# Attention by head pairs: both heads' scores side by side on TensorE, the softmax division moved behind the value product, and the batch loop written out

## What is computed

```
h = tok(x)                                   # Xnew[n] = sum over t of Wt[t, n] * x[t]
h = h + attn(layernorm(h))                   # attn normalises its input once more
h = h + ffn(layernorm(h))

xn  = (x - mu) / sqrt(var + 1e-05) * gamma + beta
q, k, v = three projections, each followed by a 3-tap convolution along the tokens
sim = q @ k.T - slope[head] * abs(i - j), masked to j <= i
out = softmax(sim) @ v
return out @ wout.T
```

## Time and profile before

| what | us |
|---|---|
| median of three runs | 1566.63 |
| the profiled execution's own time | 1568.55 |
| its span, first to last instruction | 1566.8 |
| PE busy in the span | 1354.8 |
| PE weight loads | 1089.1 |
| DVE busy | 952.7 |
| ACT busy | 671.4 |
| POOL busy | 264.4 |

### The profile page before, as it was taken

How to read it: one execution, slowest core, us unless ns; L and a number is a source line. 1 busy time by engine, 2 the same in 40 slices (tenths; PEclk the granted TensorE clock), 3 DMA queues, 4 the chain that set the end, 5 groups by cost and what they waited for, 6 DMA issues and landing times. The chain is left out here.

```text
span 1566.8 us, 26688 instructions
## 1 busy us (share of the span) xinstructions
PE 1354.8 (86%) x7905; PEld 1089.1 (70%) x7905; DVE 952.7 (61%) x3107; ACT 671.4 (43%) x1759; POOL 264.4 (17%) x262
## 2 busy tenths in 40 slices
PE   6999999999369999989999899999997896466663
PEld 5999999999356777766767667677665685355553
DVE  3433434334569898879878798788874566621211
ACT  2334334333235655656546565456653341021211
POOL 6000000000010001001110000100000400178885
PEclk9999999999679999999999999999998898687877
DMA  4000000000100000000000000000000112044542
GB/s 106 17 15 20 20 10 20 20 10 20 35 11 10 2 22 23 22 21 17 10 17 21 21 20 10 14 21 12 12 12 20 28 34 60 6 79 81 97 82 39
DMA packets 93851, 43.86 MB, mean 28 GB/s; under 512 B 31295, under 2 KB 90088, under 8 KB 93752
## 3 DMA queue, kind: packets, MB, share of 16 engines
q1 hardware_dynamic: 69960, 36.25, 8.5%
q0 software_dynamic: 23808, 6.69, 3.3%
HBM read 29.52 MB, written 10.18 MB: 25 GB/s over the span
## 5 line engine op out<-in xcount | busy, mean ns | idle before, releaser
L783 ACT ACTIVATE P<-P,nmax 125x375 f32<-125x375 f32 (+2 forms) x384 | 189.1, 494 | 292.1 <-DVE nmax L923 291.9
L287 PE MATMUL bank<-h1hl,W2hl 128*128 128x376 f32 x1536 | 278.0, 336 | 2.9 <-DVE h1hl L402 2.9
L287 PEld LDWEIGHTS bank<-h1hl,W2hl 128*128 128x128 f32 x1536 | 264.0, 189 | 3.1 <-DVE h1hl L402 3.1
L624 PE MATMUL bank<-QK 64*125 64x375 f32 (+2 forms) x768 | 197.8, 391 | 13.4 <-DVE nmax L923 13.4
L624 PEld LDWEIGHTS bank<-QK 64*125 64x125 f32 x768 | 112.8, 185 | 75.8 <-DVE nmax L923 25.0
L364 ACT ACTIVATE h<-bank,b2c 128x375 f32<-128x375 f32 x128 | 73.5, 574 | 207.3 <-PE bank L287 207.3
L923 DVE CUSTOM_DVE_ANT_0 P<-bank,nbias 125x375 f32<-125x375 f32 (+2 forms) x384 | 139.7, 413 | 2.6 <-PE bank L624 2.5
L1569 ACT ACTIVATE hE<-bank,EB 128x375 f32<-128x375 f32 x64 | 36.7, 573 | 199.0 <-PE bank L1544 196.4
L680 PE MATMUL bank<-WVT,xnThl 128*125 128x512 f32 x432 | 115.7, 413 | 3.0 <-DVE QK L972 3.0
L913 DVE TENSOR_SCALAR P<-P,prec 125x375 f32<-125x375 f32 (+2 forms) x384 | 111.9, 347 | 4.5
L865 POOL TENSOR_SCALAR lnve<-lnmv 125x3 f32<-125x3 f32 x32 | 10.1, 315 | 575.6 <-DVE lnmv L891 575.6
(11 more groups left out here) (196 smaller groups left out, 2363.4 us busy)
## 6 DMA issues: line engine op xcount, KB each, us to landing
X<-in_x_dram SPq DMA_DIRECT2D x34, 375.0 KB
EW<-in_L_ffn_w_dram SPq DMA_DIRECT2D x32, 256.0 KB
token_table<-row SPq DMA_DIRECT2D x16, 210.9 KB
tTall<-tT SPq DMA_DIRECT2D x16, 187.5 KB, 2.3
out_dram<-oS SPq DMA_DIRECT2D x16, 187.5 KB
tTall<-in_L_tok_W_dram SPq DMA_DIRECT2D x1, 1024.0 KB, 7.1
EB<-in_L_ffn_b_dram SPq DMA_DIRECT2D x16, 62.5 KB
tok<-token_table,ids POOLq DMA_INDIRECT x48
```

The costliest lines, as they stand in the source:

```text
L287: last = nc.tensor.matmul(bank[4 + m % 2][:, :NE], W2hl[:, a, k, m * 128:(m + 1) * 128], h1hl[:, p, b, k], start=(k == 0 and n == 0), stop ...
L624: last = nc.tensor.matmul(bS[unit][:PT_, at:at + w], QK[r:r + DH, 0, c, i * PT_:(i + 1) * PT_], QK[r:r + DH, 1, c, :w], start=True, stop=True)
L783: nc.scalar.activation(P[:, h % 4, SEG[q]:SEG[q] + w], P[:, h % 4, SEG[q]:SEG[q] + w], ACT.Exp, bias=nmax[:, h % 4, q:q + 1], scale=-1.0, ...
```

## The change

Attention now goes by pairs of heads. A body still has eight steps, two for each pair c = h // 2: part 0 has the 375-wide score block of both heads, part 1 the 250- and the 125-wide blocks of both. In each, the matmul of the even head (array rows 0 to 63, bank bS[0]) is followed by that of the odd head (rows 64 to 127, bank bS[1]).

`P` is no longer multiplied by the reciprocal. The six row sums of a pair get one small reciprocal (`prec`, 6 elements a row), which a copy widens over 64 channels and both heads (`precw`, 384 elements). PE transposes `precw` with three more transposes per pair into columns 375 to 499 of the bT banks, ScalarE copies them into `PT` with the probabilities, and DVE multiplies the attended values by them when it takes them out of bO into `OT`; ScalarE's copy of bO is gone. All four copies of transposed probabilities of a pair are ScalarE's now, three of them 500 wide. The transposes read 128 columns of `P` where they read 125. They and `attend` stand one pair and two pairs behind the scores.

The two norms in a row before the attention become one with a combined variance term; `n1`, nine instructions on it and six of its statistics are gone. GpSimd subtracts and multiplies for both remaining norms (two 384-element operations each) and computes `cellmax`, which has two buffers now. The loop in `bodies` is gone: b = -3 to 17 is straight code, and waits are on constants.

Cut to what the text speaks of (indented 12 columns less):

```diff
-LOOP0, LOOP1 = 3, 13
-SEG = (0, N, N + PT_)
-ORDER = (2, 0, 1)
-LN = 9
+SEG = (N, N + PT_, 0)
+LN = 7
+PW = 2 * N + 3
+TW = N + PT_
...
-P = sb_("P", [PT_, 4, 2 * N])
+P = sb_("P", [PT_, 4, PW])
-psum_ = sb_("psum_", [PT_, 4, NT])
-prec = sb_("prec", [PT_, 4, NT])
-PT = sb_("PT", [PT_, 4, 2 * N])
+psum_ = sb_("psum_", [PT_, 2, NT, 2])
+prec = sb_("prec", [PT_, 2, NT, 2])
+precw = sb_("precw", [PT_, 2, NT, 2, DH])
+PT = sb_("PT", [128, 2, 4, TW])
...
 def bodies(eng, body):
-    for b in range(FIRST, LOOP0):
-        body(b, b % 2)
-    with eng.Fori(LOOP0, LOOP1 - 1, 2) as i:
-        body(i, LOOP0 % 2)
-        body(i + 1, (LOOP0 + 1) % 2)
-    for b in range(LOOP1, LAST + 1):
+    for b in range(FIRST, LAST + 1):
         body(b, b % 2)
...
+def pair_before(b, c, back):
+    return b + (c - back) // 4, (c - back) % 4
+PARTS = ((2,), (1, 0))
+ORDER = ((2, 0), (2, 1)), ((1, 0), (0, 0), (1, 1), (0, 1))
...
+    def scores(b, c, part):
+        n = 4 * b + c
         pe.wait_ge(s_qk, 8 * b + 2 * c + 2)
-        for unit, tiles in enumerate(((2,), (0, 1))):
-            wait(pe, s_s, 3 * (8 * b + h) - 2 + 2 * unit)
-            for i in tiles:
-                w, at = (i + 1) * PT_, 0 if i != 1 else PT_
-                last = nc.tensor.matmul(bS[unit][:PT_, at:at + w],
+        wait(pe, s_s, 6 * n + 2 * part)
+        for i in PARTS[part]:
+            w, at = (i + 1) * PT_, 0 if i else 2 * PT_
+            for q in range(2):
+                r = DH * q
+                last = nc.tensor.matmul(bS[q][:PT_, at:at + w],
                                         QK[r:r + DH, 0, c, i * PT_:(i + 1) * PT_],
                                         QK[r:r + DH, 1, c, :w], start=True, stop=True)
-            last.then_inc(s_sp, 1)
...
+        last.then_inc(s_sp, 1)
+    def transpose_probs(b, c, q):
+        n, r = 4 * b + c, c % 2
+        if q == 0:
+            pe.wait_ge(s_ex, 6 * n + 6)
+        for half, blocks in enumerate((((0, 0), (1, 0), (2, 0)), ((1, 1), (2, 1), (2, 2)))):
+            wait(pe, (s_pt0, s_pt1)[half], 2 * n + q)
+            for k, (i, j) in enumerate(blocks):
+                f = SEG[i] + j * PT_
+                last = nc.tensor.transpose(bT[half][:, k * PT_:(k + 1) * PT_],
+                                           P[:, 2 * r + q, f:f + 128], ident[:PT_, :PT_])
+            i = 2 * q + half - 1
+            if i >= 0:
+                if i == 0:
+                    pe.wait_ge(s_rc, 2 * n + 2)
+                last = nc.tensor.transpose(bT[half][:, N:TW],
+                                           precw[:, r, i].rearrange("p q d -> p (q d)"),
+                                           ident[:PT_, :PT_])
+            last.then_inc(s_tp, 1)
     def attend(b, c, u):
-        pe.wait_ge(s_pt0, 8 * b + 2 * c + 2)
-        pe.wait_ge(s_pt1, 8 * b + 2 * c + 2)
+        n, r = 4 * b + c, c % 2
+        pe.wait_ge(s_pt0, 2 * n + 2)
+        pe.wait_ge(s_pt1, 2 * n + 2)
         pe.wait_ge(s_v, 3 * b + 3)
-        wait(pe, s_o, 4 * b + c)
-        for j, at in enumerate((0, N, 2 * N - PT_)):
-            for h in (2 * c, 2 * c + 1):
-                r, w = DH * (h % 2), N - j * PT_
-                last = nc.tensor.matmul(bO[r:r + DH, j * PT_:N], V[:, u, j, h * DH:(h + 1) * DH],
-                                        PT[:, h % 4, at:at + w], start=(j == 0), stop=(j == NT - 1))
+        wait(pe, s_o, n)
+        for j in range(NT):
+            half, at, w = min(j, 1), (j // 2) * 2 * PT_, N - j * PT_
+            for q in range(2):
+                last = nc.tensor.matmul(bO[DH * q:DH * (q + 1), j * PT_:N],
+                                        V[:, u, j, (2 * c + q) * DH:(2 * c + q + 1) * DH],
+                                        PT[:PT_, r, 2 * q + half, at:at + w],
+                                        start=(j == 0), stop=(j == NT - 1))
         last.then_inc(s_pv, 1)
...
             if valid(b):
-                scores(b, h)
-            if h < 2 and valid(b - 1):
-                transpose_probs(b - 1, HEADS - 2 + h)
-            if h >= 2 and valid(b):
-                transpose_probs(b, h - 2)
+                scores(b, c, part)
             if h == 0 and valid(b):
                 project_qk(b, 3, u)
             if isinstance(b, int) and (b, h) == (-1, 0):
                 pe.wait_ge(s_wl, len(split_weights))
                 pe.wait_ge(s_wh, len(split_weights) + 1)
-                pe.wait_ge(s_pad, 3)
+                pe.wait_ge(s_pad, 4)
             p = projection_step(b, h)
             if p in (2, 4, 6) and valid(b + 1):
                 project_qk(b + 1, p // 2 - 1, v_)
+            m, d = pair_before(b, c, 1)
+            if valid(m):
+                transpose_probs(m, d, part)
+            m, d = pair_before(b, c, 2)
+            if part == 0 and valid(m):
+                attend(m, d, u if c >= 2 else v_)
...
+    def exps(b, c, part):
+        n, r = 4 * b + c, c % 2
+        for k, (i, q) in enumerate(ORDER[part]):
+            w = (i + 1) * PT_
+            act.wait_ge(s_s, 6 * n + 2 * part + k + 1)
+            nc.scalar.activation(P[:, 2 * r + q, SEG[i]:SEG[i] + w], P[:, 2 * r + q, SEG[i]:SEG[i] + w],
+                                 ACT.Exp, bias=nmax[:, 2 * r + q, i:i + 1], scale=-1.0,
+                                 accum_out=psum_[:, r, i, q:q + 1]).then_inc(s_ex, 1)
+    def copy_probs(b, c, q):
+        n, r = 4 * b + c, c % 2
+        wait(act, s_o, n - 1)
+        for half, w in enumerate((TW if q else N, TW)):
+            act.wait_ge(s_tp, 4 * n + 2 * q + half + 1)
+            nc.scalar.copy(PT[:, r, 2 * q + half, 0:w], bT[half][:, :w]
+                           ).then_inc((s_pt0, s_pt1)[half], 1)
...
+            if part == 1 and valid(m):
+                copy_probs(m, d, 1)
             if valid(b):
-                n = 8 * b + h
+            if part == 0 and valid(m):
+                copy_probs(m, d, 0)
...
+    def rsqrt(ve, r, mv, grow_, eps, s, n):
+        nc.gpsimd.tensor_scalar(ve[:], mv[:, :, 1], grow_, eps, ALU.mult, ALU.add).then_inc(s, 1)
+        pool.wait_ge(s, n + 1)
+        nc.gpsimd.tensor_tensor(r[:], ve[:], mhalf[:], ALU.pow).then_inc(s, 1)
+    def ln_apply(dst, m, mv, r, s, n):
+        nc.gpsimd.tensor_tensor(dst[:, :, 0:C], Hall[:, m], mv[:, :, 0:1].broadcast_to([PT_, NT, C]),
+                                ALU.subtract).then_inc(s, 1)
+        pool.wait_ge(s, n + 3)
+        nc.gpsimd.tensor_tensor(dst[:, :, 0:C], dst[:, :, 0:C],
+                                r[:, :, None].broadcast_to([PT_, NT, C]), ALU.mult).then_inc(s, 1)
+            if h == 1 and valid(b + 2):
+                m = b + 2
+                wait_apart(pool, s_lnd, LN * (m + 1), s_on[1])
+                rsqrt(lnve, lnr, lnmv, 1.0 + EPS, EPS * EPS, s_lnp, 4 * m)
+                wait(pool, s_xtp, m)
+                ln_apply(n2, m, lnmv, lnr, s_lnp, 4 * m)
+            if h >= 2 and valid(b + 3):
+                m, k = b + 3, h - 2
+                wait_apart(pool, s_csb, m + 1, s_on[1])
+                wait_apart(pool, s_ov, 6 * m + k - 1, s_on[1])
+                nc.gpsimd.tensor_scalar(cellmax[:, k % 2], grid0[:], csb[:, TT_ + k:TT_ + k + 1], None,
+                                        ALU.max).then_inc(s_cm, 1)
             if h == 4 and valid(b - 1):
                 m = b - 1
-                rsqrt(gve, gr, gmv, s_gp, 2 * m, s_g, (LN + 1) * m + 7)
+                wait_apart(pool, s_g, LN * (m + 1), s_on[1])
+                rsqrt(gve, gr, gmv, 1.0, EPS, s_gp, 4 * m)
+                wait(pool, s_tab, 16 * m)
+                wait(pool, s_ttp, m)
+                wait(pool, s_pp, m)
+                ln_apply(row, m, gmv, gr, s_gp, 4 * m)
     bodies(pool, body)
@@ -890,46 +922,62 @@
             wait_apart(dve, s, n + t + 1, s_on[0])
             nc.vector.bn_aggr(mv[:, t], stat[:, t]).then_inc(s, 1)
...
+    def biased_max(b, c, part):
+        n, r = 4 * b + c, c % 2
+        if part == 0:
+            wait(dve, s_tp, 4 * (n - 1))
+        wait_apart(dve, s_sp, 2 * n + part + 1, s_on[0])
+        for i, q in ORDER[part]:
+            w, at = (i + 1) * PT_, 0 if i else 2 * PT_
+            nc.vector.tensor_tensor_reduce(
+                out=P[:, 2 * r + q, SEG[i]:SEG[i] + w], in0=bS[q][:PT_, at:at + w],
+                in1=nbias[:, 2 * c + q, (2 - i) * PT_:N], scale=1.0, scalar=MASKED, op0=ALU.add,
+                op1=ALU.min, accum_out=nmax[:, 2 * r + q, i:i + 1]).then_inc(s_s, 1)
...
-                    nc.vector.tensor_scalar(P[:, hh, SEG[q]:SEG[q] + w], P[:, hh, SEG[q]:SEG[q] + w],
-                                            prec[:, hh, q:q + 1], None, ALU.mult).then_inc(s_pn, 1)
+            m, d = pair_before(b, c, 2)
+            if part == 1 and valid(m):
+                n = 4 * m + d
+                dve.wait_ge(s_pv, n + 1)
+                wait(dve, s_wo, m)
+                nc.vector.tensor_tensor(OT[:, d].rearrange("p (t i) -> p t i", i=PT_),
+                                        bO[:, :N].rearrange("p (t i) -> p t i", i=PT_),
```

(19 more changed lines are left out.)

187 lines of the change are left out of this document (53 added, 134 removed).

## The result

The changed kernel takes **1475.93 us** (median of 4 runs, 1474.93 to 1477.27) against 1566.65 before: ratio 0.942, interval 0.9404 to 0.9437, or 90.7 us less. The prediction's own list of what would be wrong ends with "bodies under 41 us"; they are 40.8, so its walk of a body failed in part.

A forecast was written before the change was run, and what follows sets the result against it. PE was taken to bound stage two, DVE close behind. Work of 39.7 plus 1.1, 0.5 and 0.85 gave 42.2 us a body; sixteen bodies save 73.5, so 1568.55 - 73.5 - 1.9 gives 1493 us, range 1462 to 1540.

The forecast's parts named there:

- bodies under 41 us: Stage two: last sign listed as proving the prediction wrong; its own walk had 42.2 us a body.
- the loop: Stage two's batch loop: twelve bodies fall from 569.5 us to 12 x 44.8, saving 32 us.
- PE's work: PE in a stage-two body: 44.8 less 0.8 of waits, less 5.6, plus 1.3, giving 39.7 us.
- scores, a body: PE's scores: row halves overlap fully, a pair takes 1.53 instead of 2.92 us, saving 5.6 us a body.
- transposes of `precw`, a body: PE: three more transposes per pair, 12 a body at 0.106 us each, adding 1.3 us.
- wait for `precw`: PE in step 2: `precw` is there at 14.05, PE's transpose at 12.9, adding 1.1 us a body.
- wait for OT: PE before the output projection: OT is ready at 17.7, wanted at 17.2, adding 0.5 us a body.
- half clock: PE's clock: one half-clock stretch in every second body, adding 0.85 us a body, bounds 0 and 1.7.
- rival of no overlap: PE's scores: row halves do not run side by side; 45.8 us a body, 1551 us; chance 0.12.
- a rival, for `overlap`: DVE's `overlap` waits for POOL's second `cellmax`, OT comes 1.2 us later; 44.25 us a body, 1526 us; chance 0.18.
- Counted as whole: Stage two's ends: sixteen batches reckoned, with the shorter last bodies counted at full share.
- everything answers in time: Stage two: waits stay like those of before; 40.3 us a body, 1463 us; chance 0.18.

The follow-up runs named there:

- e1: The kernel before with its batch loop written out as straight code and nothing else changed: 1528.03 us, ratio 0.9756 to the kernel before.
- e2: The changed kernel with the loop of two-batch turns put back: 1510.3 us, ratio 0.965 to the kernel before.
- e3: The changed kernel with the odd head's scores moved away from the even head's on PE: 1653.78 us, ratio 1.0567 to the kernel before.
- e8: The changed kernel with DVE's `pTs` copy and OT multiplication earlier, plus ScalarE's copy of V ahead of `Wt`: 1461.6 us, ratio 0.9333 to the kernel before.
- e5: The changed kernel with DVE's copy of `pTs` ahead of the input norm's statistics: 1479.35 us, ratio 0.9447 to the kernel before.
- e6: The changed kernel with DVE's copy of `pTs` ahead of the input norm's statistics and its OT multiplication ahead of `overlap`: 1468.88 us, ratio 0.9382 to the kernel before.

## Why the prediction was right, and where its sizes were off

Its two large terms hold in kind, the loop and the heads side by side, and so does PE's work. The walk of the waits does not: of the three small terms it added, one is a third of its size and two are nothing, and two waits that are there it did not name. The terms, in the order of the sum:

| term | predicted | measured | from |
|---|---|---|---|
| the loop, twelve bodies | -32 | -37.8 (back in: +34.2) | e1, e2 |
| waits of before, a body | -0.8 | -0.8 | e1 |
| scores, a body | -5.6 | -4.9 | e1, after, e3 |
| transposes of `precw`, a body | +1.3 | +1.3 | e1, after |
| PE's other work, a body | 0 | -0.2 | e1, after |
| wait for `precw` | +1.1 | +0.35 | after |
| wait for OT | +0.5 | 0 | after |
| wait for V | none | +0.55 | after, e8 |
| wait for `pTs` | none | +0.25 | after, e5, e6 |
| half clock | +0.85 | 0 | after |
| a body against a straight one of before | -2.6 | -3.48 | 40.84 against 44.32 |

- **The loop** was the largest miss in one term. The step "twelve straight ones would take 12 x 44.8" took for the straight level a stretch whose last 18.8 us run in the loop; straight bodies settle at 44.3 (e1). That the jump brings DVE's stall and a wait of PE was right. Against straight bodies, the four bodies with a jump are 6.9 to 7.9 us longer (51.2 to 52.2), 29.6 together, and the other bodies that touch the loop give the remaining 8.2. Why DVE stands in "issue" at a jump no run here shows.
- **Scores.** "Full overlap, as the nearest row" was right (e3), where the rival of no overlap had 0.12. "1.42 + 0.11 = 1.53" was 1.7 (1.68 in the steps above, 6.82 / 4 over a body): the entry was priced from transposes, and cutting the scores in two costs some 0.2.
- **PE's work**, 39.7 a body, came out at 39.7, and that is luck: the start was 0.5 too high, the scores 0.7 too good, and 0.2 of other work went that the sum did not have.
- **The wait for `precw`.** DVE's side of the walk held: `precw` predicted at 14.05 from step 0, there at 634.57 + 0.70 - 621.32 = 13.95. PE's side did not: "PE reaches its transpose at 12.9" was 13.7 (635.33 - 0.35 - 621.32), since it had waited 0.25 for `pTs` and its own steps were 0.5 longer. A wait is the difference of two arrivals, and an error of 0.8 in either is most of it. What makes this wait is not the reason given either: DVE's copy takes 0.70 beside POOL's operation and would take 0.36 without. The prediction had put POOL and DVE in each other's way into a rival, for `overlap`, and priced the copy at up to 0.56.
- **The wait for OT.** Predicted OT 17.7 and PE 17.2; measured 17.25 (638.57 - 621.32) and 17.43. POOL's 384-wide operations took 0.83 and not 0.96, and the first `cellmax` was there half a us earlier. The chain is real and has 0.2 to spare: e5 delays it, and PE waits 0.6.
- **V and `pTs`** I did not walk. Both are answers of an engine that is far from full. ScalarE is busy 29 of 41 us, and its copy of V still stands behind four exponentials and `Wt`, while PE is back at that bank after one piece of scores (611.55, with the wait behind it, at 613.00).
- **The clock.** The price of a half-clock stretch was charged for a wait of 1.1 that is 0.35; the longest wait in a body is 0.55, and the clock stays at 1.00, as it did with waits of 0.45 before.
- **The ends.** "Counted as whole" gave the four other bodies 4 x 2.6 = 10.4; ahead of and behind the twelve, 13.9 came off.

Together: 5.8 for the loop, 10.3 for the twelve bodies (531.7 - 490.2 = 41.5, where 12 x 2.6 = 31.2 was predicted), 3.5 for the ends and 0.4 in stage three are the 20.1, but for rounding, by which the span's saving of 93.6 passed the predicted 73.5. Of the rivals, "everything answers in time" (40.3 a body) was closest in its body and still not the case: 1.15 us of waits are there, and e8 shows that 0.8 of it could go. POOL and DVE do stand in each other's way: by 0.3 us on `overlap`, which had that much room, and by 0.34 on the copy to `precw`, which had none.

The other parts of the change (the division moved behind the value product, the merged norms, what GpSimd does of the norms) no run takes back alone. With `cellmax` they took 10.7 us a body from DVE (40.3 to 29.6). DVE was busy for 40.3 of 44.8 us, so with that work left no body could have been shorter than 40.3; what the change would have brought without them is not shown.
